# Laying out the query and key weights by (place in the head, head), and filling the attention stacks with six loads a unit

## What is computed

```python
x = x + attn_a(layernorm(x), Wqkv, bqkv, Wo, bo)     # one head of 128
x = x + ffn(layernorm(x), qweight, scale, zero, bias)
x = x + attn_b(layernorm(x), wq, wk, wv, wo)         # 32 heads of 16, rotary, causal
x = x + ffn(layernorm(x), qweight, scale, zero, bias)
```

```python
q = (x @ wq).reshape(b, s, 32, 16); k = (x @ wk).reshape(b, s, 32, 16)
# rotary: neighbours x[..., 2i], x[..., 2i+1] of a head are turned by cos, sin of the position
o0 = x0 * c - x1 * s;  o1 = x0 * s + x1 * c
scores = einsum('bqhd,bkhd->bhqk', q, k) / sqrt(16)   # causal, softmax over k, times v, times wo
```

## Time and profile before

| | us |
|---|---|
| median of three runs (273.1 to 275.1) | 274.35 |
| the profiled execution, its own time | 273.97 |
| its span, first to last instruction | 272.2 |
| TensorE busy | 254.4 |
| VectorE busy | 224.4 |
| GpSimd busy | 182.2 |
| ScalarE busy | 145.0 |

### The profile page before, as it was taken

One profiled execution on the slowest core, in us unless ns is written; L12 is line 12 of the kernel. 1 busy time (PEld: TensorE's weight loads), 2 busy tenths in 40 slices (PEclk: granted clock), 3 DMA queues, 4 the chain that ended last, 5 costly groups with the idle time before them and its releaser, 6 DMA issues.

```text
span 272.2 us, 6539 instructions
## 1 busy us (share of the span) xinstructions
PE 254.4 (93%) x2363; PEld 213.5 (78%) x2363; DVE 224.4 (82%) x402; ACT 145.0 (53%) x239; POOL 182.2 (67%) x229
## 2 busy tenths in 40 slices
PE   7699999998989999999899999997999999999964
PEld 2597887896888987888798898885868876785744
DVE  3682679497798989899888899987988999966976
ACT  2749996644546073457443478526433683268030
POOL 5578978998798495954858587495665552475070
PEclk9999999999999999999999999999999999999999
DMA  7998170203454336334333533531634531102012
GB/s 214 294 392 297 36 198 4 77 2 94 140 147 140 92 91 168 109 88 112 103 113 108 149 94 94 146 107 45 182 111 122 158 87 52 40 3 79 31 68 98
DMA packets 51192, 31.86 MB, mean 117 GB/s; under 512 B 5400, under 2 KB 46552, under 8 KB 51160
## 3 DMA queue, kind: packets, MB, share of 16 engines
q1 hardware_dynamic: 51160, 31.44, 38.8%
HBM read 22.91 MB, written 8.39 MB: 115 GB/s over the span
## 4 chain that ended last, share of the span: by engine, by line
PE 30%; POOL 16%; SPq 15%; DVE 14%; issue 9%; ACT 8%; DMA 7%; DVEq 0%; ACTq 0%; POOLq 0%
SPq L490 13%; PE psum L885 5%; PE psum L886 5%; PE psum L887 5%; PE psum L1052 3%; POOL rstd L543 3%; DVE stats L759 3%; PE psum L1037 3%; DMA QK<-qk_parts 3%; DMA qk_parts<-parts 2%; POOL X L556 2%; DVE XT_lo L764 2%; ACT E L718 2%; PE psum L1015 2%; POOL SH L576 2%
## 5 line engine op out<-in xcount | busy, mean ns | idle before, releaser
L588 POOL TENSOR_SCALAR_AFFINE_SELECT E<-E 128x512 f32<-128x512 f32 x64 | 40.7, 661 | 36.8 <-ACT E L718 36.8
L718 ACT ACTIVATE E<-psum 128x1536 f32<-128x1536 f32 x32 | 46.4, 1449 | 26.3 <-PE psum L1039 19.5
L838 DVE TENSOR_REDUCE nmax<-psum 128x4 f32<-128x512 f32 (+1 forms) x64 | 59.1, 939 | 0.7 <-PE psum L1015 0.6
L885 PE MATMUL psum<-XT_lo,wb_hi 128*128 128x256 f32 x128 | 37.7, 294 | 0.0
L886 PE MATMUL psum<-XT_hi,wb_lo 128*128 128x256 f32 x128 | 36.2, 283 | 0.0
L887 PE MATMUL psum<-XT_hi,wb_hi 128*128 128x256 f32 x128 | 36.1, 282 | 0.0
L622 ACT ACTIVATE XN<-X,offset,rstd 128x512 f32<-128x512 f32 x30 | 24.1, 809 | 19.6 <-POOL offset L544 19.5
L764 DVE TENSOR_TENSOR XT_lo<-psum,XT_hi 128x512 fp32r<-128x512 f32 x32 | 21.5, 683 | 15.6 <-ACT XT_hi L595 15.5
L595 ACT ACTIVATE parts<-SH 128x512 bf16<-128x512 f32 x32 | 19.9, 626 | 25.4 <-POOL SH L581 14.1
L885 PE MATMUL psum<-wb_lo,XT_hi 128*128 128x256 f32 (+1 forms) x96 | 32.6, 339 | 0.0
L1015 PE MATMUL psum<-QK 128*128 128x128 bf16 x256 | 28.8, 220 | 3.1 <-DMA QK<-qk_parts 3.1
(11 more groups left out here) (104 smaller groups left out, 677.5 us busy)
## 6 DMA issues: line engine op xcount, KB each, us to landing
QK<-qk_parts SPq DMA_DIRECT2D x192, 64.0 KB
qk_parts<-parts SPq DMA_DIRECT2D x16, 384.0 KB, 2.8
X<-L_attn_a_x SPq DMA_DIRECT2D x8, 256.0 KB, 4.7
out<-X SPq DMA_DIRECT2D x6, 256.0 KB, 2.4
wb_raw<-L_attn_b_wq SPq DMA_DIRECT2D x1, 1024.0 KB, 11.0
wb_raw<-L_attn_b_wk SPq DMA_DIRECT2D x1, 1024.0 KB, 11.4
wb_raw<-L_attn_b_wv SPq DMA_DIRECT2D x1, 1024.0 KB, 11.9
QK<-mask_rows SPq DMA_DIRECT2D x8, 128.0 KB
```

What stands on the lines that cost most here:

```text
L588: last = nc.gpsimd.affine_select(out=e, in_=e, compare_op=ALU.is_ge, fill=0.0, base=0, pattern=[[0, GH], [1, P]], channel_multiplier=-1)
L718: nc.scalar.activation(E[:, n % 2], bank(3, 3), ACT.Exp, scale=float(HD) ** -0.5).then_inc(done[k], 1)
L838: nc.vector.tensor_reduce(nmax[:, u % 2, g::NG, t], (bank(1, 2) if t else bank(0)).rearrange("p (h k) -> p h k", h=GH), AX, ALU.max, negat ...
L885: nc.tensor.matmul(out_, stat[0], mov[1], start=first, stop=False)
```

## The change

`wq` and `wk` come to the kernel with their columns in another order: within each block of 128 the order (head, place) becomes (place, head). The 128 rows that a projection makes are then (place, head). Neighbours in a head are 8 rows apart, so the shuffle swaps rows by `i ^ 8` and the rotary tables are made for that order. In the scratch, the 8 heads of one place are now next to each other, 4 KB without a gap, as they stand along a row of the stack. `SL` fills the stack with six DMAs: for the blocks of rows (0, 1, 2), (3, 4) and (5), one for queries, which all hold the same part and repeat one source, and one for keys, which hold parts 0 to n - 1. The steps, the waits and the order of `PLAN` are as before; `stack_loads` counts six loads in place of twelve.

```diff
+LOADS = ((0, 3), (3, 2), (5, 1))
 KROWS = HD * len(Q_PARTS)
...
-    pair = (np.arange(P) % HD) // 2
-    sign = np.where(np.arange(P) % 2 == 0, -1.0, 1.0).astype(np.float32)
+    place = np.arange(P) // UH
+    pair = place // 2
+    sign = np.where(place % 2 == 0, -1.0, 1.0).astype(np.float32)
...
-            return 16 * (2 + (2 * len(Q_PARTS) + 1) * (u // QK_SLOTS) + 2 * len(Q_PARTS))
+            return 16 * (2 + (2 * len(LOADS) + 1) * (u // QK_SLOTS) + 2 * len(LOADS))
...
-                    for a, (stack, which) in enumerate(((queries(u), Q_PARTS), (keys(u), K_PARTS))):
-                        for row, c in enumerate(which):
-                            sp.dma_start(stack[row * HD:(row + 1) * HD],
-                                         scratch[u % 2, c, a].rearrange("(h d) t -> d h t", d=HD)
-                                         ).then_inc(qk_loaded[u % QK_SLOTS], 16)
+                    for row, n in LOADS:
+                        q, kk = (stack[row * HD:(row + n) * HD].rearrange("p h t -> p (h t)")
+                                 for stack in (queries(u), keys(u)))
+                        part = scratch[u % 2, Q_PARTS[row], 0].rearrange("(d h) t -> d (h t)", d=HD)
+                        sp.dma_start(q, part.unsqueeze(0).to_broadcast((n, HD, UH * S))
+                                     ).then_inc(qk_loaded[u % QK_SLOTS], 16)
+                        sp.dma_start(kk, scratch[u % 2, 0:n, 1].rearrange("c (d h) t -> c d (h t)", d=HD)
+                                     ).then_inc(qk_loaded[u % QK_SLOTS], 16)
...
-                    nc.vector.stream_shuffle(SH[:, u % 2], ps, [i ^ 1 for i in range(32)])
+                    nc.vector.stream_shuffle(SH[:, u % 2], ps, [i ^ UH for i in range(32)])
...
+    for n in ("L0_attn_b_wq", "L0_attn_b_wk"):
+        arrays[n] = np.ascontiguousarray(arrays[n].reshape(C, KT, UH, HD).transpose(0, 1, 3, 2).reshape(C, C))
```

## The result

The changed kernel takes 351.59 us (median of 4 runs, 349.77 to 352.37) against 274.21 us before (273.1 to 275.1). The ratio is 1.2815, with a 95% interval of 1.2743 to 1.2887: slower by 77 us. The forecast was 321 us with a range up to 342. The direction and the mechanism held; the size was too small by 30 us.

What follows compares the result with a forecast made beforehand. TensorE bounds the kernel before; after, narrow loads on 2 or 3 DMA engines do. Loads 168.0, stores 19.5 and handovers 19.8 from 66.3 delay the last scores by 46.9 us: about 321 us, range 298 to 342.

Steps and rivals of the forecast that it cites:

- What bounds the kernel: TensorE fills each unit of about 10.2 us; relief of SP, which issues the stack loads, can bring about 3.4 us.
- The parts without a price: Weights, projection, tables and shuffle by `i ^ 8` cost 0; SP issues six loads in about 2.8 us, not 5.51.
- Who carries the loads: Stack loads: a DMA divides along its outermost count, so four wide loads run on the same first 3 or 2 engines.
- The price of a piece: A 4 KB piece of the stack loads takes 159 ns; 66 on the busiest engine make 10.5 us a unit.
- The handover: Between a unit's store and the next loads the DMA queue pauses 1.8 us; a unit in strict turn costs 13.6 us.
- the correction of 4 us: In units 1, 4, 10 and 12 the second store slips partly into a handover, -4; left against +3 before unit 12.
- The sum: From 66.3, loads 168.0, stores 19.5, handovers 19.8 and landing 1.1 put the last unit's scores at 274.7, 46.9 later.
- The upper end: 10.8 us of loads a unit and handovers of 3.0 us give 339; 3 for the clock makes 342.
- 298: First rival: the DMA queue never runs dry, handovers are hidden, a unit costs 11.5 us; 298 us, 12 in 100.
- the second rival: The wide loads spread over all 16 engines, 271 us; not much slower below about 7.1 us of loads; 7 in 100.
- The third rival: Wide loads narrow but on varying engines, or only the queries' repeated source narrow: 272 to 276 us, 6 in 100.
- What was to be seen: Profile after: DMA share 0.12 to 0.19 for long stretches, TensorE's stack wait over 30 us, unit periods 13 to 14 us.

Runs made afterwards that it cites:

- the kernel with the place first: Changed kernel with rows of the wide blocks as (place, copy) in place of (copy, place), six loads whose source counts 16 first: 271.15 us.
- the twelve loads: Changed kernel with layout, tables and 4 KB pieces kept, but twelve loads of 16 rows in place of six: 272.84 us.
- The run with other rows: Changed kernel with blocks in reverse order of rows, the block of three at rows 48 to 95, the block of two at 16 to 47: 344.85 us.
- the store beside: Changed kernel with a unit's store waiting until the loads of the unit before have landed, where they stand ahead of it: 367.24 us.
- the repeated source: Changed kernel with only the queries' wide loads, which repeat one source, left narrow and the keys in loads of 16 rows: 300.40 us.
- the place of the singles: Changed kernel with the two loads of 16 rows issued ahead of the four wide ones: 352.93 us.
- the clock held up: Changed kernel with 16 thrown-away matmuls ahead of each unit's wait for its stacks: 353.98 us.
- half of the narrow load: Changed kernel with only the keys' or only the queries' wide loads left narrow, the others in loads of 16 rows: 300.84 and 300.40 us.

## Why the prediction was right in direction and wrong in size

**What bounds the kernel.** Right. Relief of SP could bring some 3.4 us; the kernel with the place first brought 2.4.

**The parts without a price.** Right for layout, tables and shuffle: 742 ns before and in the twelve loads, and no time of their own. The issue was too low: the six loads take 3.8 us of SP (271.92 to 275.74), not 2.8, since a narrow one takes up to 0.77 us to issue. It lies under the loads and costs nothing.

**Who carries the loads.** Right, and now shown by a run: 3 and 2 engines for the block first, 16 for the place first. The shares of 0.19 and 0.13 in the profile after show that the narrow loads share engines.

**The price of a piece.** 159 ns was right for a piece that runs undisturbed: it is the median of all 3072 pieces. That was in part luck: it was worked out from stretches with all 16 engines at work, and where all 16 carry these loads a piece takes 241 or 302 ns in the median (twelve loads, place first). The step that failed is the one after it, 66 pieces times that price. It takes no account of what the pieces do to each other. The loads took 12.05 us a unit and not 10.5, 24.9 us over 16 units. That is most of the miss. The run with other rows takes 10.7 us of it away (16 x 0.67), so that part hangs on which rows the engines write at once; that it is those 32 apart is argued. The other runs speak against the store beside, the repeated source, the place of the singles and the clock. The rest, some 0.9 us a unit, is largely a slow piece at the start of a group, as the one unit without it shows (10.46 us), and its cause is open.

**The handover.** In strict turn the time from the last piece of the loads, over the store, to the next first piece is 3.0 to 3.6 us, with 3.1 forecast. Before unit 12 it is 8.1 us: SP issues that store only at 241.7, when unit 12's parts are ready; on VectorE their last step stands behind the maxima of unit 10, and those behind the first scores of unit 11, at 239.4. I had allowed 3 us there, for SP's own wait for the same maxima, and had not seen that the parts hang on them too. The four second stores, 1.3 us each in the sum, left no gap of their own, which is the correction of 4 us that I had set against another. All gaps together are 41.5 us and not 39.3.

**The sum.** 66.3 for the first piece was 67.1. With 192.9 us of loads and 41.5 of gaps the last piece ends at 301.5, and the scores begin 0.5 later, at 302.0. Against the forecast's 274.7 that is 27.3: 24.9 from the loads, 2.2 from the gaps, 0.8 at the start, and 0.6 less for the landing. The tail, which I had kept at 44.4 us, is 2.7 longer. The clock is at 0.50 in its first three microseconds, which is likely part of it; with the clock held up, at 0.77 there, the same stretch to the end took 46.0 us and not 47.1:

```profile
302.00:305.00 3.00, 2.97 (x21) 2.73 (x22) 2.29 (x5) 0.19 (x1) 0.00 (x0) 0.50 0.02 5
305.00:340.00 35.00, 33.30 (x265) 24.96 (x265) 25.00 (x47) 15.85 (x25) 16.62 (x27) 0.96 0.11 38
```

27.3 and 2.7 are the 30 us.

**The upper end.** It added a dearer piece and a slow handover, each from the rows, and left nothing for pieces that disturb each other. 342 was therefore too low for a resource that had never been run alone on 3 engines.

**The rivals.** The queue did run dry, so 298 was out of reach. The loads were not spread; the kernel that spreads them is the second rival come true, and its 271 us were right. No run contradicts its threshold, 7.1 us of loads a unit, though none lies close to it. The two kernels with less (6.2 and 4.6) are not slower than before, all with more (8.6 and up) are. The third rival, that only the repeated source is narrow, falls, since the keys' loads cost as much; its figure for half of the narrow load, up to 276 us, was about 25 too low.

**What was to be seen.** The share of 0.12 to 0.19 and the wait of over 30 us came as written. The period came out longer, 14.8 us in the mean (65.5 to 288.0 over 15 units) and 16 in strict turn, not 13 to 14.

## What to carry to other kernels

Fewer and larger DMAs help only if each still reaches all DMA engines (271 us here, against 352): put a dimension that counts 16 or a multiple of it outermost on both sides, above all when a repeated or blocked source would put a 2 or 3 there. To judge such a change, count the pieces on the busiest engine and compare them with the time of a stage, not the total bytes with the total share, which fell here while the time rose by 28%. When a piece's price is taken from a stretch with all engines at work, leave room above: a queue that becomes the bound shows costs that its idle time had covered.

## What was not expected of the hardware

- While three engines carried the block of three, at rows i, i + 16 and i + 32, two of them had for part of the time pieces of about 305 ns in place of 159; with the block at rows 48, 64 and 80 on most of that was gone (135 and 52 such pieces in all). The Trainium skill (SBUF: State Buffer, Door 1, the DMA port swizzle) says that partitions 32 apart in one half of the 128 share a port, those in different halves don't. The run agrees in its direction (351.6 to 344.9 us).
- With the place first, all 16 engines write into at most 48 rows a load and moved 173 GB/s at a share of 0.86, against 399 for loads of 2 KB pieces into 128 rows at 1.06 in the earlier trace rows. A 4 KB piece took 302 ns in the median there, where the changed kernel, with 2 or 3 engines at work most of the time, had 159: so a piece cost more with all engines at work. It was hidden here, and its cause wasn't tried.
- The early store, which waits in the queue behind the loads, is still worth 16 us over issuing it afterwards (351.6 against 367.2).
- TensorE's granted clock went from 1.00 to 0.64 and 0.50 in waits of several microseconds and was back at 1.00 later. With the DMA engines as the bound, holding it up (0.961 in the mean in place of 0.907) brought no time that could be measured (354.0 us).
